# Attention inside a fused transformer layer: where the softmax division and the causal mask are done

## What is computed

```python
q, k, v = (proj(wq), proj(wk), proj(wv))          # 32 heads of 32
q = _apply_rope(q, sin, cos)
k = _apply_rope(k, sin, cos)
scores = jnp.einsum('bnth,bnsh->bnts', q, k) * (1.0 / math.sqrt(h))
scores = jnp.where(causal, scores, -jnp.inf)
attn = jax.nn.softmax(scores, axis=-1)
out = jnp.einsum('bnts,bnsh->bnth', attn, v)       # then @ wo, + x, layernorm
# feed-forward: Wg, Wu, Wd = codebook[idx] (16384 entries of 8 values)
h = jax.nn.silu(x @ Wg.T) * (x @ Wu.T)
x = _layernorm(x + h @ Wd.T)
```

## Time and profile before

| | us |
|---|---|
| median of 3 runs | 6752.01 (6750.79 to 6754.25) |
| the profiled execution | 6752.44 |
| its span, first to last instruction | 6750.5 |
| TensorE busy | 6615.4 (98%) |
| VectorE busy | 4662.0 (69%) |
| ScalarE busy | 3789.6 (56%) |
| GpSimd busy | 4927.0 (73%) |
| attention, 680 to 1537.8 us of the span | 857.8 |

### The profile page before, as it was taken

One profiled execution on the slowest core, in us unless ns is written; L12 is line 12 of the kernel. 1 busy time (PEld: TensorE's weight loads), 2 busy tenths in 40 slices (PEclk: granted clock), 3 DMA queues, 4 the chain that ended last, 5 costly groups with the idle time before them and its releaser, 6 DMA issues.

```text
span 6750.5 us, 115830 instructions
## 1 busy us (share of the span) xinstructions
PE 6615.4 (98%) x29584; PEld 4063.9 (60%) x29584; DVE 4662.0 (69%) x11407; ACT 3789.6 (56%) x6692; POOL 4927.0 (73%) x5188
## 2 busy tenths in 40 slices
PE   9999899999999999999999999999999999999998
PEld 3444566666666666666666666666666666666664
DVE  3320888886776876777667776777767777677764
ACT  0000788886666755556555555555556555555552
POOL 7777777777777777777777777777777777777772
PEclk9999999999999999999999999999999999999999
DMA  4232232233333333333333333333333333333331
GB/s 140 64 90 48 56 60 55 58 80 75 82 84 74 78 72 75 65 74 73 73 68 74 76 74 73 67 74 74 72 75 67 73 73 74 74 66 73 73 71 63
DMA packets 479940, 490.59 MB, mean 73 GB/s; under 512 B 228672, under 2 KB 349248, under 8 KB 472896
## 3 DMA queue, kind: packets, MB, share of 16 engines
q10 hardware_dynamic: 298720, 425.47, 22.5%
q0 software_dynamic: 165888, 21.57, 7.8%
q1 hardware_dynamic: 14688, 36.48, 1.4%
HBM read 426.34 MB, written 56.72 MB: 72 GB/s over the span
## 4 chain that ended last, share of the span: by engine, by line
PE 75%; ACT 1%; issue 1%; DVE 0%; DMA 0%; ACTq 0%; DVEq 0%
PE ps L427 42%; PE ps L457 18%; PE ps L476 9%; PE ps L402 3%; PE ps L438 3%; PE ps L444 1%; ACT onehot L771 0%; ACT onehot L775 0%; PE ps L413 0%; PE ps L557 0%; DVE small L1068 0%; ACT arena L866 0%; DMA out_dram<-arena 0%; DVE onehot L1018 0%; DMA arena<-code_low 0%
## 5 line engine op out<-in xcount | busy, mean ns | idle before, releaser
L216 POOL DMA_INDIRECT raw<-in_codebook_dram,idx_sb x5184 | 4926.8, 950 | 1720.6 <-DMA raw<-in_codebook_dram,idx_sb 1566.8
L1018 DVE TENSOR_SCALAR_CACHE_REDUCE onehot<-arena,small 128x512 fp32r<-128x512 f32 x3845 | 2623.4, 743 | 1049.0 <-PE ps L427 998.8
L427 PE MATMUL ps<-onehot,table 128*128 128x512 f32 x12288 | 3267.6, 417 | 23.0 <-ACT onehot L775 18.7
L427 PEld LDWEIGHTS ps<-onehot,table 128*128 128x128 f32 x12288 | 2290.7, 188 | 900.1 <-issue 353.9
L771 ACT ACTIVATE onehot<-arena,small 128x512 fp32r<-128x512 f32 x2307 | 1496.7, 713 | 1139.1 <-PE ps L427 980.1
L775 ACT ACTIVATE onehot<-onehot,small 128x512 fp32r<-128x512 f32 x2307 | 1487.4, 708 | 0.0
L457 PE MATMUL ps<-big,arena 128*128 128x512 f32 x2752 | 1267.9, 597 | 0.0
L457 PEld LDWEIGHTS ps<-big,arena 128*128 128x128 f32 x2752 | 510.2, 189 | 571.7 <-issue 543.7
L1025 DVE SCALAR_TENSOR_TENSOR picked<-arena,small,ps 128x512 f32<-128x512 f16 x768 | 572.3, 745 | 158.3 <-PE ps L438 142.2
L476 PE MATMUL ps<-arena 128*128 128x512 f32 (+1 forms) x1408 | 640.4, 600 | 1.8 <-ACT arena L744 1.2
L922 DVE TENSOR_REDUCE small<-ps 128x1 f32<-128x384 f32 (+7 forms) x512 | 374.2, 752 | 270.1 <-PE ps L321 267.5
(11 more groups left out here) (74 smaller groups left out, 2726.1 us busy)
## 6 DMA issues: line engine op xcount, KB each, us to landing
arena<-code_low ACTq DMA_DIRECT2D x770, 256.0 KB
arena<-code_high ACTq DMA_DIRECT2D x770, 128.0 KB
raw<-in_codebook_dram,idx_sb POOLq DMA_INDIRECT x5184
gathered_units<-raw SPq DMA_DIRECT2D x39, 512.0 KB
arena<-gathered_units ACTq DMA_DIRECT2D x19, 1024.0 KB
queries_keys<-arena ACTq DMA_DIRECT2D x16, 1024.0 KB, 4.0
arena<-queries_keys ACTq DMA_DIRECT2D x32, 512.0 KB
big<-queries_keys ACTq DMA_DIRECT2D x32, 512.0 KB
```

Of the source, the lines that this page charges most:

```text
L216: pool.indirect_dma_start(raw[:, s, n, :], None, codebook, bass.IndirectOffsetOnAxis(ap=idx_sb[:, s, n:n + 1], axis=0), engine_sem=describ ...
L427: last = mm(ps[:, 4 + s % 2, :], table[:, k, c, :], onehot[:, k, :], start=(k == 0 and c == 0), stop=(k == KLO - 1 and c == PIECES - 1))
L1018: dve.tensor_scalar(onehot[:, k, :], lo_sb[:, s % 2, :], kp_sb[:, k:k + 1], None, ALU.is_equal, ALU.add, accum_out=hits[:, k:k + 1]).then_ ...
```

## The change

The probabilities are no longer divided by their row sums. They are turned and weighed as they leave the exponential, so `turn` waits for `exp_done` in place of `probs_ready`, and the division is made on the weighed output, 64 x 128 per block. The output has the query along the free axis, so the reciprocals must be turned: VectorE takes one reciprocal per round over 128 x (4 x 32) elements, each sum repeated 32 times (`invert_sums`); TensorE multiplies these four 128 x 32 matrices with the unit matrix at the head of `weigh`, into the free columns of banks 4 and 5 (four f32 products); VectorE copies them to SBUF (`copy_rinv`, two copies of 64 x 128) and multiplies in place of the plain copy of the outputs (`copy_o`). The mask is no longer added by TensorE: the four bf16 products per round are gone, and VectorE adds it to the diagonal blocks of both heads in PSUM, one instruction of 128 x (2 x 128) per block (`add_mask`), before the maxima.

```diff
-        mask_sb, idb_sb = kb(60, 1)[:, P:P + P // 2].bitcast(BF16), kb(60, 1)[:, P + P // 2:2 * P].bitcast(BF16)
+        mask_sb = kb(60, 1)[:, P:2 * P]
...
-        negmax, rowsum, rinv = small[:, 34:38], small[:, 38:42], small[:, 4:8]
+        negmax, rowsum = small[:, 34:38], (small[:, 38:42], small[:, 4:8])
+        rinv = kb(61, 1).rearrange("p (r e d) -> p r e d", r=2, e=4)
+        rinv_rows = kb(60, 1)[:, 0:P]
...
                         mm(ps[:, bank + wide * n + c0 // N, 0:w], qk[r, 0, d0:L], qk[r, 1, c0:c0 + w],
-                           start=True, stop=(c0 + w < L))
-                for n in range(2):
-                    mm(ps[:, bank + wide * n + d0 // N, d0 % N:d0 % N + P], idb_sb, mask_sb,
-                       start=False, stop=True).then_inc(scores_done, 1)
+                           start=True, stop=True).then_inc(scores_done[o], 1)
...
                         if c == 0:
-                            pe.wait_ge(probs_ready, i * STEPS + (4 * u + 2 * o + n + 1))
+                            pe.wait_ge(exp_done, i * STEPS + (4 * u + 2 * o + n + 1))
...
                 if free:
                     pe.wait_ge(exp_done, i * STEPS + (4 * (u + 2) + 2))
+                pe.wait_ge(rinv_done, i * ROUNDS + (u + 1))
+                for o in range(2):
+                    for n, hh in enumerate(heads):
+                        strip = (hh + 2 * o) % HG
+                        last = mm(ps[strip * HD:(strip + 1) * HD, 5 - o, 0:P],
+                                  rinv[:, u % 2, 2 * o + n, :], id_sb[:, :], start=True, stop=True)
+                last.then_inc(rinv_turned, 1)
                 pe.wait_ge(turns_copied, i * (TURNS * ROUNDS) + (TURNS * u + 6))
...
+            def add_mask(i, u, o):
+
+                tb = round_of(u)[1][o]
+                bank, wide, d0 = 4 - 4 * o, 1 + o, tb * P
+                pieces = 2 * (tb * P // N + 1)
+                dve.wait_ge(scores_done[o], i * (pieces * ROUNDS) + (pieces * u + pieces))
+                diagonal = ps[:, bank + d0 // N:bank + d0 // N + wide + 1:wide, d0 % N:d0 % N + P]
+                dve.tensor_tensor(diagonal, diagonal, mask_sb.unsqueeze(1).to_broadcast([P, 2, P]),
+                                  ALU.add).then_inc(diagonal_masked, 1)
...
-            def normalise(i, u, e):
-                L = (round_of(u)[1][e // 2] + 1) * P
-                dve.wait_ge(exp_done, i * STEPS + (4 * u + e + 1))
-                dve.reciprocal(rinv[:, e:e + 1], rowsum[:, e:e + 1]).then_inc(rinv_done, 1)
-                dve.wait_ge(rinv_done, i * STEPS + (4 * u + e + 1))
-                dve.tensor_scalar(probs_of[u % 2][e][:, 0:L], probs_of[u % 2][e][:, 0:L], rinv[:, e:e + 1], None,
-                                  ALU.mult).then_inc(probs_ready, 1)
+            def invert_sums(i, u):
+
+                dve.wait_ge(exp_done, i * STEPS + (4 * u + 4))
+                dve.reciprocal(rinv[:, u % 2, :, :], rowsum[u % 2].unsqueeze(2).to_broadcast([P, 4, HD])
+                               ).then_inc(rinv_done, 1)
+
+            def copy_rinv(i, u):
+                dve.wait_ge(rinv_turned, i * ROUNDS + (u + 1))
+                for o in range(2):
+                    strip = (round_of(u)[0][0] + 2 * o) % HG
+                    r = slice(strip * HD, (strip + 2) * HD)
+                    dve.tensor_copy(rinv_rows[r, :], ps[r, 5 - o, 0:P]).then_inc(rinv_copied, 1)
+                dve.wait_ge(rinv_copied, i * (2 * ROUNDS) + (2 * u + 2))
...
-                dve.tensor_copy(oT[rows, bass.ds(i * T + tbs[o] * P, P)],
-                                ps[strip * HD:(strip + 2) * HD, 4 + o, 0:P]).then_inc(o_copied, 1)
...
+                r = slice(strip * HD, (strip + 2) * HD)
+                dve.tensor_tensor(oT[rows, bass.ds(i * T + tbs[o] * P, P)], ps[r, 4 + o, 0:P], rinv_rows[r, :],
+                                  ALU.mult).then_inc(o_copied, 1)
+
+            def attention_round(i, u, weighed=True, inverted=True):
+                add_mask(i, u, 0)
                 row_max(i, u, 0)
                 row_max(i, u, 1)
-                if normalised:
-                    normalise(i, u - 1, 3)
-                normalise(i, u, 0)
+                add_mask(i, u, 1)
                 row_max(i, u, 2)
-                normalise(i, u, 1)
+                if inverted:
+                    invert_sums(i, u - 1)
                 row_max(i, u, 3)
                 if weighed:
+                    copy_rinv(i, u - 2)
                     for o in range(2):
                         copy_o(i, u - 2, o)
-                normalise(i, u, 2)
```

More of the change, by code:

```diff
@@ L173, in seq_post_ln_layer @@
         qk_in = [sem(f"qk_in{p}") for p in range(HG // 2)]; far_in = [sem(f"far_in{p}") for p in range(HG // 2)]; v_in = [sem(f"v_in{p}") for p in range(HG // 2)]
-        scores_done = sem("scores_done"); negmax_done = sem("negmax_done")
-        exp_done = sem("exp_done"); rinv_done = sem("rinv_done"); probs_ready = sem("probs_ready")
+        scores_done = [sem(f"scores_done{o}") for o in range(2)]; diagonal_masked = sem("diagonal_masked"); negmax_done = sem("negmax_done")
+        exp_done = sem("exp_done"); rinv_done = sem("rinv_done"); rinv_turned = sem("rinv_turned"); rinv_copied = sem("rinv_copied")
         turns_done = sem("turns_done"); turns_copied = sem("turns_copied")
@@ L377, in _ @@
             pe.wait_ge(const_in, 16 * 6)
-            pe.wait_ge(mask_ready, 2)
             pe.wait_ge(v_copied, SB)
@@ L629, in exponent @@
                 act.activation(probs_of[u % 2][e][:, 0:L], src[:, 0:L], ACT.Exp, bias=negmax[:, e:e + 1],
-                               scale=1.0, accum_out=rowsum[:, e:e + 1]).then_inc(exp_done, 1)
+                               scale=1.0, accum_out=rowsum[u % 2][:, e:e + 1]).then_inc(exp_done, 1)
             def copy_turned(i, u, j):
@@ L878, in _ @@
             dve.tensor_copy(mask_sb, mask_raw).then_inc(mask_ready, 1)
-            dve.tensor_copy(idb_sb, id_sb[:, :]).then_inc(mask_ready, 1)
-            dve.wait_ge(mask_ready, 2)
+            dve.wait_ge(mask_ready, 1)
             dve.wait_ge(prep_in, 16 * 2)
@@ L919, in row_max @@
                 bank = (4, 5, 0, 2)[e]
-                dve.wait_ge(scores_done, i * STEPS + (4 * u + e + 1))
+                dve.wait_ge(diagonal_masked, i * (2 * ROUNDS) + (2 * u + e // 2 + 1))
                 src = ps[:, bank:bank + 1 + e // 2, :].rearrange("p h t -> p (h t)")
                 dve.reduce_max(negmax[:, e:e + 1], src[:, 0:L], AX.X, negate=True).then_inc(negmax_done, 1)
-            def normalise(i, u, e):
-                L = (round_of(u)[1][e // 2] + 1) * P
-                dve.wait_ge(exp_done, i * STEPS + (4 * u + e + 1))
-                dve.reciprocal(rinv[:, e:e + 1], rowsum[:, e:e + 1]).then_inc(rinv_done, 1)
-                dve.wait_ge(rinv_done, i * STEPS + (4 * u + e + 1))
-                dve.tensor_scalar(probs_of[u % 2][e][:, 0:L], probs_of[u % 2][e][:, 0:L], rinv[:, e:e + 1], None,
-                                  ALU.mult).then_inc(probs_ready, 1)
+            def invert_sums(i, u):
[9 more added lines that the diff above has]
+                dve.wait_ge(rinv_copied, i * (2 * ROUNDS) + (2 * u + 2))
             def copy_o(i, u, o):
@@ L936, in copy_o @@
                 dve.wait_ge(pv_done, i * (2 * ROUNDS) + (2 * u + o + 1))
-                dve.tensor_copy(oT[rows, bass.ds(i * T + tbs[o] * P, P)],
-                                ps[strip * HD:(strip + 2) * HD, 4 + o, 0:P]).then_inc(o_copied, 1)
-            def attention_round(i, u, weighed=True, normalised=True):
+                r = slice(strip * HD, (strip + 2) * HD)
[3 more added lines that the diff above has]
+                add_mask(i, u, 0)
                 row_max(i, u, 0)
                 row_max(i, u, 1)
-                if normalised:
-                    normalise(i, u - 1, 3)
-                normalise(i, u, 0)
+                add_mask(i, u, 1)
                 row_max(i, u, 2)
-                normalise(i, u, 1)
+                if inverted:
+                    invert_sums(i, u - 1)
                 row_max(i, u, 3)
                 if weighed:
+                    copy_rinv(i, u - 2)
                     for o in range(2):
                         copy_o(i, u - 2, o)
-                normalise(i, u, 2)
             with dve.Fori(0, NG) as g:
@@ L964, in _ @@
                 attention_round(PASSES - 1, u)
-            normalise(PASSES - 1, ROUNDS - 1, 3)
+            invert_sums(PASSES - 1, ROUNDS - 1)
             for u in range(ROUNDS - 2, ROUNDS):
+                copy_rinv(PASSES - 1, u)
                 for o in range(2):
```

## The result

The changed kernel takes 6832.26 us (median of 4 runs, 6828.53 to 6838.02), the kernel before 6753.13 (6750.79 to 6754.38). The ratio is 1.0117 with a 95% interval of 1.0104 to 1.013: 79 us slower. The forecast was 6794, with a range of 6760 to 6840.

What follows compares the result with a forecast made beforehand. A loop of waits through TensorE, VectorE and ScalarE in attention was taken as the bound. Four rounds would go from 26.46 to 27.76 us; +1.30 x 32 = +41.6 on 6752.44 gives 6794 us, range 6760 to 6840.

Steps and rivals of the forecast that it cites:

- the slow reciprocal: Rival: VectorE's 128-element reciprocal takes up to 1.30 us, so VectorE sets (0,7) and (1,6); 6834 us, chance 0.23.
- The path that the prediction read: In attention rounds (3,4) and (2,5), a chain through TensorE, VectorE and ScalarE sets the length: 7.20 and 6.97 us.
- The mask on VectorE: Addition before the maxima: 0.46 us with semaphore, less 0.15 from an earlier start, +0.31 us on the path.
- The four products: Eight TensorE instructions at the head of weigh, 0.21 us on the path in every round.
- The rounds: Attention's four rounds after the change: (3,4) 7.72, (2,5) 7.49, (0,7) 6.02, (1,6) 6.53 us; sum 27.76 against 26.46.
- Normalising gone: VectorE's saved work gives nothing in (2,5), (3,4) and (0,7); in (1,6) it removes a 0.28 us wait.
- the reciprocal: VectorE's reciprocal over 128 elements, taken as 0.29 us, with bounds of 0.29 and 1.30.
- the prediction's own lists: VectorE's work per round until outputs are copied: 5.78, 5.99, 6.20 and 6.41 us, below all four round lengths.
- scores would wait for the outputs in no round: Sign in the changed profile: the next round's scores never wait for VectorE's multiplied outputs.
- The first rival: VectorE's 128-element reciprocal is slow, up to 1.30 us, and bounds (0,7) and (1,6); 6834 us, chance 0.23.
- The faster rival: TensorE's own work limits attention: 0.31 us gained per round, capped by gathers past some 24 us; 6728 us, chance 0.12.
- the gathers run by themselves: GpSimd's gathers were taken as independent of attention; a later attention gives them slack.

Runs made afterwards that it cites:

- short_recip: The changed kernel with a reciprocal of 4 numbers per row in place of 128, repeated by the weight load: 6807.3 us, ratio 1.0079.
- div_short: The kernel before with the division moved to the outputs, a reciprocal of 4 numbers per row, mask still on TensorE: 6774.24 us, ratio 1.0031.
- no_division: The kernel before with reciprocals, normalising multiplications and their waits left out: 6744.34 us, ratio 0.9987.
- div_only: The changed kernel with the mask left on TensorE, long reciprocal kept: 13263.31 us on a chip where the kernel before takes 13209.
- filler: The changed kernel with the first 512 columns of the long scores computed twice in rounds (2,5) and (3,4): 6913.74 us, ratio 1.0236.
- mask_only: The kernel before with only the mask moved to VectorE, normalising kept: 6837.63 us, ratio 1.0127.
- the two full reorderings: Turns 0 and 1 put before long scores, their copies before exponentials, on the kernel before (6777.45 us) and the change with a 4-number reciprocal (6775.99 us).
- reorder_half: The kernel before with turns 0 and 1 and their copies moved ahead in rounds (2,5) and (3,4) only: 6757.54 us, ratio 1.001.

## Why the prediction was right, and where it was not

**Right:** the direction, and the range. The time of 6832 us lies in the range because this had been widened to take in the slow reciprocal; the forecast itself gave 42 of the 79 us. The path that the prediction read in (3,4) and (2,5), short scores, mask, maximum, exponentials, copy, turn, weigh, turn, held in every experiment.

- *The mask on VectorE*, taken at 0.42 us with bounds of 0.29 and 0.69, took 0.429. On the path it was put at +0.31; short_recip against div_short shows +0.34 in (2,5) and (3,4), and -0.29 in (0,7), where the prediction had -0.19. In (1,6) it shows +0.26.
- *The four products*, 0.21 us: 0.21 and 0.22 in div_short, 0.24 from the first of them to the weighing.
- *The rounds:* (3,4) 7.72 against 7.76, (2,5) 7.49 against 7.53. With the short reciprocal, which leaves VectorE's list below the path as I had assumed for the long one, the four rounds sum to 27.64; the prediction had 27.76. It started from a group whose round (1,6) took 6.29 us, though, where the median is 6.12: counted from the medians the rise is 1.34, and the prediction had 1.30.
- *Normalising gone is worth nothing* but in (1,6): no_division shows 5 us.

**Wrong: the size of one term, the reciprocal.** I took 0.29 us from rows of one element and the slope of other instructions. It is 0.942. Between 4 and 128 elements it rises by (942 - 167) / 124 = 6.25 ns per element, six times the 1.04 of the maxima. My argument that a one-element reciprocal shows no more than the fixed cost was too weak: at 6.25 ns per element in place of 1.04 a reciprocal of one element is 5 ns longer, 3% of its 154, and the argument cannot see that. With 0.86 back to back in place of 0.21, the prediction's own lists give 6.43 for (0,7) and 6.64 for (1,6); measured 6.46 and 6.71. The sign that it had named for this came too: the prediction said that scores would wait for the outputs in no round, and 30 of 31 rounds (0,7) end in such a wait (0.55 us in the median) and 27 of 31 rounds (1,6) (0.09). div_only shows the same without the mask addition. The first rival was the right one in its mechanism, and its 6834 lay 2 us from the result, though partly by luck: its reciprocal of 1.30 us was too long, and it had nothing for the clock. The Trainium skill's sentence on a repeat count of 8 ("VectorE: DVE Perf Modes", "Walkthrough: the 8-slice pipeline in each mode") pointed the right way; read as eight cycles it says 1.22 us, and the row says 0.942.

**Not in the prediction: the clock.** The medians explain (28.46 - 26.30) x 31 groups = 67 us. Seven half-clock stretches of 3.4 us in attention, where the kernel before has none after its start, raise the mean of four rounds from 28.46 to 28.80, another 10.5: the 24 groups without one take 28.45 us in the mean, the 7 others 30.00. The three rounds ahead of these groups took 1.3 us more (28.4 against 27.2). Together that is 79. One of the stretches (columns as in the earlier trace rows; the clock is the figure behind the busy times):

```profile
799.10:802.40 3.30, 3.30 (x42) 2.69 (x41) 1.98 (x5) 2.43 (x7) 2.69 (x3) 0.50 0.08 4
```

Five of the seven began in a round (3,4), just behind the 1.47 us for which TensorE had idled there, and two in (1,6), just behind an idle time of 1.00. Filler, which took 0.86 of the 1.47 away, had none in (3,4) and two in (1,6). All 6 of short_recip and all 15 of mask_only lie in (3,4), again behind 1.47 us of idle time; those of the two full reorderings lie in (1,6), behind the waits of 0.8 to 1.4 us at the end of (0,7). But (2,5), in which TensorE idles 1.24 us in the changed kernel, had none, and most rounds (3,4) had none either. What the exact condition is stays open.

By parts, in us per four rounds: products +0.69 net of VectorE's relief in (1,6), mask on VectorE +0.65, long reciprocal +0.82. The parts are not additive by edit, though: put on the kernel before, the mask costs 1.99 per four rounds (mask_only) in place of 0.65, since with the normalising in it VectorE's list has no room for the mask. Moving the division made that room and paid 20 us for it. That mask_only ends 5 us behind the whole change goes with the clock: the groups without a half-clock stretch take 28.45 us in both, but mask_only has 15 with one where the change has 7.

**The faster rival's cap was wrong too.** I gave a gain 24 us until the gathers bind, from the last gather and TensorE's use of it. reorder_half shows that an earlier hand-over, that of the last pair of gathered weights, binds first. And the sentence that the gathers run by themselves was wrong: in the changed kernel, without the normalising, they end 26 us earlier, which would have given the faster rival more room and not less.

## What to carry to other kernels

Find the loop of waits before counting work: here VectorE was 86% busy in its stage and taking 41% of its work away was worth 5 us, while 0.34 us put onto the loop in each of two of the four rounds is 22 us (32 x 0.68). Do not extrapolate a duration from a one-element row of an operation of another kind: take the reciprocal of few numbers and let something else repeat them (the weight load did so at no cost). Before speeding up a stage, look at who else delivers to the end: a gain of 23 us vanished in a stream of gathers that TensorE did not wait for until it was early. And split a round's median by the granted clock before explaining it: a round of 7.47 us was one of 6.17 with a half-clock stretch in it.

## What the hardware showed that I had not expected

- A reciprocal costs VectorE about 6.25 ns per element and partition: 154 ns for 1, 167 for 4, 942 for 128.
- TensorE's clock falls to half for 3.4 us at a time in a stage where TensorE's products fill 82% and it idles 1 to 1.5 us in places; with more work in the idle time (filler) 2 such stretches are left of 7. A group of four rounds with one in it was 1.0 to 1.6 us longer.
- GpSimd's gathers take 994 ns beside VectorE's multiplication of the probabilities and 943 otherwise; over attention that puts them some 24 us behind.
- With instructions added in one loop, another that was not touched took 91 us more, in idle times of 2.7 to 4.1 us per turn that end for no reason in the trace; that the one caused the other is not shown. A total must be split by stage before it is believed.
